# A six-layer windowed attention: query norms moved into the exponentials, masks in 64x32 tiles, x turned by one transpose, feed-forward weights loaded later, and a new order of stages

## The chip, the cores and the metric

One core of one Trainium2 chip runs the whole program. The metric is the device time of one execution in microseconds, as the median of a few runs. TensorE (PE), VectorE (DVE), ScalarE (ACT), GpSimd (POOL) and the DMA queue that SyncE (SP) feeds work side by side. They wait for each other by semaphores only.

## The reference

`x` has 16 batches of 128 rows of 128 numbers. A cross attention, a mixture of experts and a second cross attention come first. Most of the work is in what follows, six layers of local attention and a gated feed-forward part:

```python
def attn_layer(x, Wqkv, qs, ksc, Wo):
    q, k, v = jnp.split(x @ Wqkv, 3, -1)          # 16 heads of 64
    q = l2norm(q) * qs
    k = l2norm(k) * ksc
    q = q * cos * scale + rotate_half(q) * sin * scale
    k = k * cos * inv + rotate_half(k) * sin * inv
    return local_attention(q, k, v) @ Wo           # windows of 32 rows, each sees itself and the one before
for i in range(DEPTH):                             # 6
    x = attn_layer(shift_tokens(x), Wqkv[i], ...) + x
    x = ffn_layer(shift_tokens(x), ln_g[i], ...) + x
```

`shift_tokens` moves columns 64 to 127 down by one row. `l2norm` divides each head's row by its norm.

## The kernel before

**Units and slots.** A layer's attention is 64 units: 16 batches times 4 groups of four heads. Each engine has a list of stages, `(skew, function)`, and in slot c it runs each stage for unit c - skew, in the order of the list. Slots 0 to 7 of a layer are written out (`start`, mixed into the feed-forward part of the layer before), slots 8 to 63 are a loop of seven iterations with eight slots each (`steady`), and the last seven slots are written out again (`finish`), mixed into the layer's own feed-forward part. So there are 42 iterations of that loop in all. An engine runs its slot strictly in order; `wait_ge` makes it wait.

**One unit.** PE turns x once per batch (`l_turn_x`, every fourth slot, L802 and L803: two products, one with the identity and one with a shifted identity, which also does `shift_tokens`), ACT copies it out of PSUM and DVE takes the rest (`xs_part`, a high and a low part). PE projects queries and keys into bank 0 (`l_project_qk`, L814) and values into bank 1 (`l_project_v`, L823), with three products each. ACT squares bank 0 (L1186), DVE sums the squares (L1594) and multiplies bank 0 with the rotary tables (L1580, L1584). POOL adds the two halves (`l_add`, L530), finds the inverse norms in four small steps (`l_norm`, from a guess that ACT makes with Ln and Exp, L1192 and L1197) and multiplies queries and keys by them (`l_scale`, L551). PE turns the result in bank 2 (`l_turn_qk`, L831), ACT copies it out (L1202), and PE makes the scores in banks 3 and 4 (`l_scores`): first two products of the identity with the mask, in bf16 over the whole array (L850), then 16 products in tiles of 64 rows by 32 columns (L858). DVE takes the negated maxima (L1602), ACT makes four exponentials with them as bias (L1166), PE turns these (`l_turn`, L841), ACT copies them (L1174), PE multiplies them with the values in 64x32 tiles (`l_pv`, L878), DVE divides (L1617, L1619), PE turns the result (`l_turn_o`, L888), ACT copies it (L1208), and PE multiplies it with Wo (`l_output`, L898). Matrix products in fp32 stand in the trace as two records each.

**Values moved by DMA.** A product in a 64x32 tile reads its weights and data from the same half of the partitions. So for each pair of units SP waits for `v_done` and copies parts of `l_v` to other partitions (`move_values`, four DMAs, L360), and `l_pv` waits for them (`moved`).

**SP's order.** In each layer SP serves the moves, the next x (`take_x`, one DMA) and, at the start of a layer, the next projection weights. At a layer's end it loads Wo and the first two x of the next layer, waits until all four groups of the feed-forward part are done (`y_done`), and loads the next layer's feed-forward weights (`load_feed_forward`, 12 DMAs, L336 to L347) before it comes to the first moves.

Of the kernel before, what the change touches and what calls it, by code (L numbers as in the profile page):

```python
# [90 lines left out]
def build(nc, t, out):  # L91
    with ExitStack() as ctx:
# [31 lines left out]

        l_mask = sb("l_mask", [128, 2 * BAND], BF16)
# [88 lines left out]
        l_rn = sb("l_rn", [128, 2, 8])  # L214
# [52 lines left out]
        l = stage_sems("l_", core.replace("sub_done ", "") + "w_high_done w_split "  # L267
# [18 lines left out]
        def _(sp):  # L286
# [21 lines left out]
            for w in range(WINDOWS):  # L308
                first = max(w - 1, 0) * WINDOW
                rows = slice(w * WINDOW, (w + 1) * WINDOW)  # L310
                for p in range(2):
                    sp.dma_start(l_mask[rows, p * BAND:(p + 1) * BAND],
                                 t["const_bf"][rows, 128 + first:128 + first + BAND]).then_inc(ld_c, 16)
# [49 lines left out]
            def take_x(ly, b, k):  # L363

                sp.dma_start(xin[:, k], one(Y, b)).then_inc(ld_xin[k], 16)
# [6 lines left out]
            def serve_layer(ly, last):  # L372

                for b in range(4):
                    for q in range(2):
# [16 lines left out]
                if not last:  # L392
# [13 lines left out]
            load_feed_forward(0)  # L406
# [16 lines left out]
        def _(pool):  # L423
# [5 lines left out]
            pool.memset(l_ss[:, :, :, 1:], 1e-24).then_inc(preset, 1)  # L429
# [93 lines left out]
            def attention(ly):  # L523
# [8 lines left out]
                def l_norm(u, b, j):  # L532
# [11 lines left out]
                    pool.tensor_tensor(l_rn[:, k], t, y, ALU.mult).then_inc(l["rn_done"], 1)  # L544

                def l_scale(u, b, j):
# [3 lines left out]
                    v = l_qk[:, k].rearrange("p (h n) -> p h n", n=L_DIM)  # L550
                    pool.tensor_tensor(v, v, l_rn[:, k, :, None].broadcast_to([128, 8, L_DIM]),  # L551
                                       ALU.mult).then_inc(l["qk_done"], 1)

                return Pipeline(pool, [(4, l_norm), (3, l_add), (4, l_scale)], UNITS, UNROLL, 4)
# [36 lines left out]
        def _(pe):  # L591
# [180 lines left out]
            def attention(ly):  # L772
# [11 lines left out]
                def values_read(mine, b, r):  # L784

                    v, x = (issued(mine, fn, r) for fn in (l_project_v, l_turn_x))
                    pe.wait_ge(l["v_done"], upto(ub, no_more(4 * b + v, UNITS)))
                    pe.wait_ge(l["x_split"], upto(bb, no_more(b + (x + 3) // 4, B)))

# [5 lines left out]

                def l_turn_x(u, b, j):

                    if j % 4 == 0:
                        x = xin[:, j // 4]
                        pe.wait_ge(ld_xin[j // 4], (ly * B + b - j // 4) * 8 + 16)  # L800
                        values_read(l_turn_x, b, 0)
# [16 lines left out]
                def l_project_v(u, b, j):  # L818
                    g = j % 4
                    pe.wait_ge(l["x_split"], upto(bb, b + 1))  # L820
                    values_read(l_project_v, b, j % 4)
# [5 lines left out]
                def l_turn_qk(u, b, j):  # L827
                    pe.wait_ge(l["qk_done"], upto(ub, u + 1))
                    pe.wait_ge(l["qkT_done"], upto(ub, u))
# [15 lines left out]
                def l_scores(u, b, j):  # L845
# [963 lines left out]
```

## Time and profile before

| what | value |
|---|---|
| median of three runs | 2391.66 us (2388.51 to 2394.93) |
| the profiled execution | 2385.23 us, span of the core 2383.4 us |
| mean granted clock of TensorE | 0.968 of full speed |
| busy share PE, DVE, ACT, POOL | 93%, 72%, 66%, 59% |

The span runs from the first to the last instruction on the core. A busy share is an average over parts with different limits, so it doesn't name the bound of a part. The layers begin at about 570 us and take some 307 us each.

### The profile page before, as it was taken

How to read it: one execution, taken by the hardware profiler on the slowest of the kernel's cores; microseconds unless marked ns; L12 is line 12 of the kernel's file. 1: busy time of each engine (PE TensorE's matmuls, PEld its weight loads, DVE VectorE, ACT ScalarE, POOL GpSimd, SP SyncE). 2: the span in 40 equal slices, each digit the busy share in tenths (PEclk: the TensorE clock that was granted, in tenths of full speed). 3: DMA queues.
4: the chain of work that ended last, by engine and by line, in shares of the span. 5: the costliest groups of instructions: out<-in, count | busy, mean ns of one | idle time of the engine just before them, and what ended most of it. 6: DMA issues, size and time to landing. Idle time of an engine off the chain costs nothing.

```text
span 2383.4 us, 105405 instructions
## 1 busy us (share of the span) xinstructions
PE 2211.0 (93%) x36645; PEld 1694.9 (71%) x36645; DVE 1725.2 (72%) x4617; ACT 1563.0 (66%) x5192; POOL 1412.3 (59%) x2638
## 2 busy tenths in 40 slices
PE   6998699998999979999799998999988999889998
PEld 4775277776888658886578875788756888578885
DVE  4777788886777657786577865677756788568884
ACT  3554455565888548886478873788746888468883
POOL 3443611115888538885378863688726888278882
PEclk9998899998999989999999999999998999999999
DMA  3000000011111112111111111211102111021110
GB/s 98 0 0 1 0 1 0 0 48 43 49 39 40 31 42 54 40 40 33 43 50 40 40 29 34 63 40 39 34 21 71 40 39 38 14 50 40 40 38 22
DMA packets 107749, 82.51 MB, mean 35 GB/s; under 512 B 26422, under 2 KB 100292, under 8 KB 107588
## 3 DMA queue, kind: packets, MB, share of 16 engines
q1 hardware_dynamic: 107588, 80.46, 12.9%
q8 instruction: 89, 1.46, 0.3%
q14 instruction: 72, 0.59, 0.1%
HBM read 21.94 MB, written 1.05 MB: 10 GB/s over the span
## 4 chain that ended last, share of the span: by engine, by line
PE 74%; DVE 4%; issue 4%; SPq 2%; ACT 1%; POOL 1%; DMA 0%; DVEq 0%; ACTq 0%; POOLq 0%
PE bank L814 14%; PE bank L831 9%; PE bank L898 7%; PE bank L878 6%; PE bank L858 6%; PE bank L823 6%; PE bank L888 4%; PE bank L841 3%; PE bank L850 2%; PE bank L749 2%; PE bank L955 2%; PE bank L944 2%; PE bank L945 2%; PE bank L738 2%; PE bank L597 1%
## 5 line engine op out<-in xcount | busy, mean ns | idle before, releaser
L530 POOL TENSOR_TENSOR l_qk<-l_rot 128x512 f32<-128x512 f32 x384 | 494.4, 1287 | 134.0 <-PE bank L831 60.6
L1202 ACT ACTIVATE l_qkT<-bank 128x512 f32<-128x512 f32 x384 | 229.8, 599 | 278.2 <-PE bank L831 278.2
L1580 DVE TENSOR_TENSOR l_rot<-bank,l_tab 128x512 f32<-128x512 f32 x384 | 265.0, 690 | 197.8 <-ACT l_sq L1186 197.8
L551 POOL TENSOR_TENSOR l_qk<-l_qk,l_rn 128x512 f32<-128x512 f32 x384 | 400.9, 1044 | 0.9
L1166 ACT ACTIVATE prob<-bank,peak 128x64 f32<-128x64 f32 x1536 | 355.0, 322 | 1.3 <-DVE peak L1602 1.3
L814 PE MATMUL bank<-w_high,xs_part 128*128 128x512 f32 x768 | 351.8, 458 | 3.2 <-DVE xs_part L1571 2.8
L1186 ACT ACTIVATE l_sq<-bank 128x512 f32<-128x512 f32 x384 | 237.1, 617 | 55.9 <-PE bank L814 44.8
L1584 DVE TENSOR_TENSOR l_rot<-bank,l_tab 128x512 f32<-128x512 f32 x384 | 261.5, 681 | 0.0
L831 PE MATMUL bank<-const,l_qk 128*128 128x128 f32 x1536 | 255.2, 289 | 5.3 <-POOL l_qk L551 5.2
L1594 DVE TENSOR_REDUCE l_ss<-l_sq 128x8 f32<-128x512 f32 x384 | 259.8, 677 | 0.2
L898 PE MATMUL bank<-l_wo,l_oT 128*128 128x128 f32 x1536 | 239.0, 279 | 0.0
L823 PE MATMUL bank<-w_high,xs_part 128*128 128x256 f32 x768 | 202.9, 286 | 11.6 <-issue 11.6
L878 PE MATMUL bank<-l_v,probT 64*32 64x65 f32 x4608 | 179.5, 225 | 35.2 <-DMA stash<-l_v 22.8
L898 PEld LDWEIGHTS bank<-l_wo,l_oT 128*128 128x128 f32 x1536 | 206.3, 193 | 3.3 <-issue 0.3
L1602 DVE TENSOR_REDUCE peak<-bank 128x4 f32<-128x256 f32 x384 | 160.8, 419 | 50.7 <-PE bank L858 43.4
L831 PEld LDWEIGHTS bank<-const,l_qk 128*128 128x128 f32 x1536 | 163.5, 142 | 41.4 <-POOL l_qk L551 6.8
L878 PEld LDWEIGHTS bank<-l_v,probT 64*32 64x32 f32 x4608 | 117.2, 108 | 105.3 <-issue 105.3
L814 PEld LDWEIGHTS bank<-w_high,xs_part 128*128 128x128 f32 x768 | 146.8, 191 | 62.2 <-issue 5.8
L435 POOL TENSOR_SCALAR ln_rs<-ln_mv 128x1 f32<-128x1 f32 (+1 forms) x64 | 14.5, 227 | 273.5 <-DVE ln_mv L1548 128.3
L858 PE MATMUL bank<-l_qkT 64*32 64x64 f32 x12288 | 175.8, 223 | 0.0
L878 PE MATMUL bank<-stash,probT 64*32 64x65 f32 x7680 | 174.5, 226 | 0.0
L1619 DVE TENSOR_TENSOR o<-bank,rsum 128x256 f32<-128x256 f32 x384 | 163.1, 425 | 13.3
(202 smaller groups left out, 5374.8 us busy)
## 6 DMA issues: line engine op xcount, KB each, us to landing
stash<-l_v SPq DMA_DIRECT2D x768, 65.0 KB, 2.0
early<-in_L_ffn_Wqkv_dram SPq DMA_DIRECT2D x36, 256.0 KB, 3.2
xin<-Y SPq DMA_DIRECT2D x96, 64.0 KB, 1.8
l_wo<-in_L_ffn_Wo_dram SPq DMA_DIRECT2D x6, 512.0 KB, 3.8
f_w<-in_L_ffn_W_dram SPq DMA_DIRECT2D x6, 341.0 KB
out_dram<-X SPq DMA_DIRECT2D x4, 256.0 KB, 2.3
f_w<-in_L_ffn_W_dram SPq DMA_DIRECT2D x6, 128.0 KB
l_oT<-in_L_xattn_Wkv_dram SPq DMA_DIRECT2D x1, 512.0 KB, 6.1
```

The source lines that it names most:

```text
L530: pool.tensor_tensor(l_qk[:, k], l_rot[:, k, 0], l_rot[:, k, 1], ALU.add).then_inc(l["add_done"], 1)
L551: pool.tensor_tensor(v, v, l_rn[:, k, :, None].broadcast_to([128, 8, L_DIM]), ALU.mult).then_inc(l["qk_done"], 1)
L814: ins = pe.matmul(bank[:, 0, :].rearrange("p (q n) -> p q n", q=2), xs_part[:, part, j // 4], w[:, 0:2, 256 * g:256 * g + 256], start=n == ...
L823: ins = pe.matmul(bank[:, 1, 0:256], xs_part[:, part, j // 4], w[:, 2, 256 * g:256 * g + 256], start=n == 0, stop=n == 2)
L831: ins = pe.transpose(bank[:, 2, n * 128:(n + 1) * 128], l_qk[:, j % 2, n * 128:(n + 1) * 128], ident)
L858: ins = pe.matmul(bank[w * WINDOW:(w + 1) * WINDOW, 3 + r, BAND * p:BAND * (p + 1)], l_qkT[rows, j % 2, queries:queries + WINDOW], l_qkT[r ...
L878: ins = pe.matmul(bank[w * WINDOW:(w + 1) * WINDOW, 6 - p, at:at + L_DIM + 1], probT[rows, j % 2, 128 * r + w * WINDOW:128 * r + (w + 1) * ...
L898: ins = pe.matmul(bank[:, 7, 256:384], l_oT[:, j // 4, p], l_wo[:, p], start=p == 0, stop=p == 7, skip_group_check=True)
L1166: ins = act.activation(prob[:, k, n * BAND:(n + 1) * BAND], bank[:, 3 + r, p * BAND:(p + 1) * BAND], ACT.Exp, bias=peak[:, k, n:n + 1])
L1580: dve.tensor_tensor(l_rot[:, k, 0].rearrange("p (q h n) -> p q h n", q=2, h=4), bank[:, 0, :].rearrange("p (q h n) -> p q h n", q=2, h=4), ...
L1584: dve.tensor_tensor(l_rot[:, k, 1].rearrange("p (q h s n) -> p q h s n", q=2, h=4, s=2), bank[:, 0, :].rearrange("p (q h s n) -> p q h s n ...
L1594: dve.tensor_reduce(l_ss[:, k, :, 0], l_sq[:].rearrange("p (h n) -> p h n", n=L_DIM), AX.X, ALU.add)\
```

## The change

1. **Query norms.** POOL's `l_scale` multiplies the keys alone, 128x256 in place of 128x512. The queries' inverse norms go into the exponentials: ACT's four `ACTIVATE`s get a `[128, 1]` scale operand beside the bias. DVE writes the negated maxima into spare columns of bank 3 and multiplies them by the inverse norms in a new small instruction (`l_shifts`). `l_rn` has four buffers instead of two, and the last step of `l_norm` waits for `exp_done` of four units before.
2. **Mask in tiles.** The two whole-array mask products become eight products in the same 64x32 tiles as the scores, each with 64 rows of the identity and 128 columns of the mask.
3. **x.** The DMA of x does the shift: two DMAs per batch. PE turns x with one transpose into bank 2, columns 384 to 511, where `l_turn_qk` also writes; each of the two waits until the other's result is read.
4. **Feed-forward weights** of a layer are loaded inside that layer, after the moves of batch 3.
5. **Order.** New stage lists on PE, ACT, DVE and POOL. Scores move from skew 5 to 4, values, squares and rotation from 1 to 2, POOL's add from 3 to 4.

```diff
             def take_x(ly, b, k):
-                sp.dma_start(xin[:, k], one(Y, b)).then_inc(ld_xin[k], 16)
+                x = one(Y, b)
+                sp.dma_start(xin[:, k, 0:HALF], x[:, 0:HALF]).then_inc(ld_xin[k], 16)
+                sp.dma_start(xin[1:, k, HALF:], x[0:S - 1, HALF:]).then_inc(ld_xin[k], 16)
...
                             load_projections(ly + 1, 2 * b + q)
+                load_feed_forward(ly)
                 with sp.Fori(2, B // 2 - 1) as i:
...
                         take_x(ly + 1, b, b)
-                    sp.wait_ge(f["y_done"], upto(0, (ly + 1) * 4))
-                    apart(sp)
-                    load_feed_forward(ly + 1)
...
-                return Pipeline(pool, [(4, l_norm), (3, l_add), (4, l_scale)], UNITS, UNROLL, 4)
+                return Pipeline(pool, [(4, l_add), (4, l_norm), (4, l_scale)], UNITS, UNROLL, 4)
...
-                        pe.matmul(bank[0:HALF, 1, 256:384], x[:, 0:HALF], ident, start=True, stop=True)
-                        pe.matmul(bank[HALF:, 1, 256:384], x[:, HALF:], shift_t, start=True, stop=True)\
-                          .then_inc(l["x_turned"], 1)
+                        pe.wait_ge(ld_xin[j // 4], (ly * B + b - j // 4) * 16 + 32)
+                        turns_read(l_turn_x, b, 0)
+                        pe.transpose(bank[:, 2, 384:512], xin[:, j // 4], ident).then_inc(l["x_turned"], 1)
...
-                    for r in range(2):
-                        pe.matmul(bank[:, 3 + r, 0:2 * BAND], ident_bf, l_mask[:], start=True, stop=False,
-                                  skip_group_check=True)
+                    apart(pe)
+                    for w in range(WINDOWS):
+                        for r in range(2):
+                            rows = slice(64 * r, 64 * r + 64)
+                            at = 64 * r + min(w, 1) * WINDOW
+                            pe.matmul(bank[w * WINDOW:(w + 1) * WINDOW, 3 + r, 0:2 * BAND],
+                                      ident_bf[rows, at:at + WINDOW], l_mask[rows], start=True, stop=False,
+                                      skip_group_check=True)
...
-                stages = [(5, l_scores), (4, l_turn_qk), (6, l_pv), (1, l_project_qk), (1, l_project_v), (7, l_output), (6, l_turn_o), (5, l_turn), (0, l_turn_x)]
+                stages = [(4, l_turn_qk), (2, l_project_v), (6, l_pv), (7, l_output), (0, l_turn_x),
+                          (1, l_project_qk), (4, l_scores), (5, l_turn), (6, l_turn_o)]
...
                                                  bank[:, 3 + r, p * BAND:(p + 1) * BAND], ACT.Exp,
-                                                 bias=peak[:, k, n:n + 1])
+                                                 bias=peak[:, k, n:n + 1],
+                                                 scale=l_rn[:, j % 4, 2 * p + r:2 * p + r + 1])
...
+                return Pipeline(act, [(1, l_copy_x), (2, l_square), (3, l_log), (6, l_copy_prob), (7, l_copy_o),
+                                      (3, l_guess), (4, l_copy_qk), (5, l_exp), (2, l_copy_v)], UNITS, UNROLL, 4)
...
+                    dve.tensor_reduce(peaks, scores, AX.X, ALU.max, negate=True).then_inc(l["peaked"], 1)
+
+                def l_shifts(u, b, j):
+                    dve.wait_ge(l["peaked"], upto(ub, u + 1))
+                    dve.wait_ge(l["rn_done"], upto(ub, u + 1))
                     dve.wait_ge(l["exp_done"], upto(ub, u - 1))
...
+                                      l_rn[:, j % 4, 0:4].rearrange("p (b a) -> p a b", a=2), ALU.mult)\
+                       .then_inc(l["shifts_done"], 1)
```

On PE, one slot of the loop without an x, before; the nine rows of `l_pv` (L878) are cut to the first two:

```order
L850 MATMUL bank<-l_mask,cbf 128x128 x2
L858 MATMUL bank<-l_qkT 32x64 x16
L831 MATMUL bank<-const,l_qk 128x128 x4
L878 MATMUL bank<-l_v,probT 32x65
L878 MATMUL bank<-stash,probT 32x65
...
L814 MATMUL bank<-w_high,xs_part 128x512
...
L823 MATMUL bank<-w_high,xs_part 128x256
...
L898 MATMUL bank<-l_wo,l_oT 128x128 x2
L888 MATMUL bank<-const,o 128x128 x2
L841 MATMUL bank<-const,prob 128x128 x2
```

The same slot of the change (its line numbers: L834 is `l_turn_qk`, L826 `l_project_v`, L886 `l_pv`, L906 `l_output`, L817 `l_project_qk`, L857 and L866 `l_scores`, L844 `l_turn`, L896 `l_turn_o`):

```order
L834 MATMUL bank<-const,l_qk 128x128 x4
L826 MATMUL bank<-w_high,xs_part 128x256
...
L886 MATMUL bank<-l_v,probT 32x65
L886 MATMUL bank<-stash,probT 32x65
...
L906 MATMUL bank<-l_wo,l_oT 128x128 x2
L815 REGISTER_ALU
L817 MATMUL bank<-w_high,xs_part 128x512
...
L857 MATMUL bank<-l_mask,cbf 32x128 x8
L866 MATMUL bank<-l_qkT 32x64 x16
L844 MATMUL bank<-const,prob 128x128 x2
L896 MATMUL bank<-const,o 128x128 x2
```

There are two tiled blocks in a slot in both. Behind them stood `l_turn_qk` and `l_project_qk`; now `l_output` and `l_turn` do, and the masks are inside the tiled block. The scores of a unit now come in the slot in which it is turned.

On SP, between the last layer's end and the first moves of the next, before (the DMAs of `f_w`, `f_g` and `f_b` in the middle are cut):

```order
L333 DMA l_wo<-in_L_ffn_Wo_dram 128x8x128
L396 ISA
L365 DMA xin<-Y 128x128 x2
L400 ISA
L336 ISA
L336 DMA f_w<-in_L_ffn_W_dram 128x682
...
L347 DMA f_b<-in_L_ffn_b_dram 128x128
L411 REGISTER_ALU
L411 COMPARE_AND_BRANCH
L360 DMA stash<-l_v 64x260 x4
```

In the change these DMAs stand behind the moves (L361) of batch 3, ahead of the loop over the later batches:

```order
L361 DMA stash<-l_v 64x260 x4
L372 REGISTER_ALU
L368 DMA xin<-Y 128x64
L369 DMA xin<-Y 127x64
L355 REGISTER_ALU
L361 DMA stash<-l_v 64x260 x4
L337 ISA
L337 DMA f_w<-in_L_ffn_W_dram 128x682
```

What moved is the whole group of 12 loads, from ahead of a layer's first moves to behind its eighth group of moves.

## Rows read from the trace of the kernel before

**Rows 1.** The page's first part: busy time, share of the span, instructions

```profile
PE 2211.0 (93%) x36645; PEld 1694.9 (71%) x36645; DVE 1725.2 (72%) x4617; ACT 1563.0 (66%) x5192; POOL 1412.3 (59%) x2638
```

**Rows 2.** Windows: stretch, us, busy (x) PE PEld DVE ACT POOL, PEclk, DMA share, GB/s

```profile
950.02:980.21 30.19, 30.02 (x681) 24.30 (x682) 24.12 (x61) 24.58 (x91) 24.73 (x49) 1.00 0.15 40
```

**Rows 3.** Timeline of PE, one slot without x: start us, us, instruction

```profile
999.56 0.50 PE L814 MATMUL bank<-w_high,xs_part 128*128 128x512 f32 x1
999.89 0.40 PE L814 MATMUL bank<-w_low,xs_part 128*128 128x512 f32 x1
...
1000.36 0.28 PE L823 MATMUL bank<-w_high,xs_part 128*128 128x256 f32 x1
...
1000.71 0.61 PE L898 MATMUL bank<-l_wo,l_oT 128*128 128x128 f32 x4
...
1001.37 0.38 PE L841 MATMUL bank<-const,prob 128*128 128x128 f32 x2
1001.59 0.28 PE L850 MATMUL bank<-l_mask,cbf 128*128 128x128 bf16 x2
1001.79 0.45 PE L858 MATMUL bank<-l_qkT 64*32 64x64 f32 x32
1002.18 0.66 PE L831 MATMUL bank<-const,l_qk 128*128 128x128 f32 x4
...
1002.77 0.24 PE L878 MATMUL bank<-l_v,probT 64*32 64x65 f32 x1
...
1003.16 0.50 PE L814 MATMUL bank<-w_high,xs_part 128*128 128x512 f32 x1
```

**Rows 4.** Timeline of PE around the turn of an x

```profile
997.30 0.38 PE L841 MATMUL bank<-const,prob 128*128 128x128 f32 x2
...
997.98 0.28 PE L850 MATMUL bank<-l_mask,cbf 128*128 128x128 bf16 x2
```

**Rows 5.** ACT and DVE in the same slot (timeline), and two ACT lines' durations

```profile
999.77 0.92 ACT L1166 ACTIVATE prob<-bank,peak 128x64 f32<-128x64 f32 x4
...
1001.41 0.24 ACT L1197 ACTIVATE l_y<-l_y 128x8 f32<-128x8 f32 x1
1001.57 0.38 ACT L1208 ACTIVATE l_oT<-bank 128x256 f32<-128x256 f32 x1
1001.85 0.38 ACT L1174 ACTIVATE probT<-bank 128x256 f32<-128x256 f32 x1
1002.87 0.60 ACT L1202 ACTIVATE l_qkT<-bank 128x512 f32<-128x512 f32 x1 [0.64 <-PE bank L831]
...
1003.42 0.18 DVE L1617 RECIPROCAL rsum<-bank 128x4 f32<-128x4 f32 x1
...
L1166 ACT ACTIVATE prob<-bank,peak 128x64 f32<-128x64 f32 x1536 | 355.0, 322 | 1.3 <-DVE peak L1602 1.3
...
L1227 ACT ACTIVATE f_ge<-bank,f_b x72: 682/687/689, 814.0 to 2374.8; 128x512 f32<-128x512 f32 x48, 85x512 f32<-85x512 f32 x24
...
L1219 ACT ACTIVATE f_nT<-bank,f_g x24: 771/777/778, 807.8 to 2365.3; 128x512 f32<-128x512 f32 x24
```

**Rows 6.** POOL's scaling, a group of the page (count | busy, mean ns)

```profile
L551 POOL TENSOR_TENSOR l_qk<-l_qk,l_rn 128x512 f32<-128x512 f32 x384 | 400.9, 1044 | 0.9
```

**Rows 7.** Waits over the span: waiting line and its releaser, total us, times, longest

```profile
PE bank L878 <- DMA stash<-l_v: 22.8, 5, 4.9
```

**Rows 8.** SP's timeline and the chain at the start of layer 1

```profile
862.77 0.35 SPq L336 DMA_DIRECT2D f_w<-in_L_ffn_W_dram  x1
...
870.28 2.43 SPq L360 DMA_DIRECT2D stash<-l_v  x4
...
872.12 2.07 DMA stash<-l_v
...
886.81 0.28 PE L850 MATMUL bank<-l_mask,cbf 128*128 128x128 bf16 x2 [4.10 <-issue]
```

**Rows 9.** Windows: PE between its two waits at the start of layer 1 (columns: rows 2)

```profile
874.30:882.70 8.40, 8.38 (x126) 6.64 (x126) 4.22 (x11) 3.87 (x12) 3.09 (x6) 0.63 0.49 138
```

More of the change, by code:

```diff
@@ L307, in _ @@
             sp.dma_start(c_wo, t["L1_xattn_Wo"].rearrange("(c p) n -> p c n", p=128)).then_inc(ld_c, 16)
[L308 to L313, printed above, removed]
+            for r in range(2):
+                for w in range(2):
+                    rows = slice(64 * r + w * WINDOW, 64 * r + (w + 1) * WINDOW)
+                    for p in range(2):
+                        sp.dma_start(l_mask[rows, p * BAND:(p + 1) * BAND],
+                                     t["const_bf"][w * WINDOW:(w + 1) * WINDOW, 128:128 + BAND]).then_inc(ld_c, 16)
             for k, n in enumerate(("gamma_x", "beta_x", "gamma_l", "beta_l")):
@@ L374, in serve_layer @@
                 for b in range(4):
+                    if b == 2:
+                        sp.wait_ge(f["y_done"], upto(0, ly * 4))
+                        apart(sp)
                     for q in range(2):
@@ L820, in l_project_v @@
                     pe.wait_ge(l["x_split"], upto(bb, b + 1))
-                    values_read(l_project_v, b, j % 4)
+                    pe.wait_ge(l["v_done"], upto(ub, u))
                     for n, (part, w) in enumerate(passes):
@@ L828, in l_turn_qk @@
                     pe.wait_ge(l["qk_done"], upto(ub, u + 1))
-                    pe.wait_ge(l["qkT_done"], upto(ub, u))
+                    turns_read(l_turn_qk, b, j % 4)
                     for n in range(4):
@@ L848, in l_scores @@
                     pe.wait_ge(l["exp_done"], upto(ub, u))
-                    for r in range(2):
-                        pe.matmul(bank[:, 3 + r, 0:2 * BAND], ident_bf, l_mask[:], start=True, stop=False,
-                                  skip_group_check=True)
+                    apart(pe)
+                    for w in range(WINDOWS):
+                        for r in range(2):
+                            rows = slice(64 * r, 64 * r + 64)
[3 more added lines that the diff above has]
+                                      skip_group_check=True)
                     for p in range(2):
@@ L1007, in _ @@
             pe.wait_ge(c["kvT_done"], upto(0, B))
-            pe.wait_ge(c["v_done"], upto(0, 2 * B))
             first.start(0)
@@ L1011, in _ @@
             pe.wait_ge(c["evac_done"], upto(0, UNITS))
+            pe.wait_ge(c["v_done"], upto(0, 2 * B))
             first.start(1)
@@ L1154, in l_copy_x @@
                         act.wait_ge(l["v_proj"], upto(ub, u - 4))
-                        act.activation(xs_part[:, 0, j // 4], bank[:, 1, 256:384], ACT.Copy)\
+                        act.activation(xs_part[:, 0, j // 4], bank[:, 2, 384:512], ACT.Copy)\
                            .then_inc(l["x_high_done"], 1)
@@ L1570, in l_split_x @@
                         dve.wait_ge(l["x_high_done"], upto(bb, b + 1))
-                        dve.tensor_tensor(xs_part[:, 1, k], bank[:, 1, 256:384], xs_part[:, 0, k].bitcast(F32), ALU.subtract)\
+                        dve.tensor_tensor(xs_part[:, 1, k], bank[:, 2, 384:512], xs_part[:, 0, k].bitcast(F32), ALU.subtract)\
                            .then_inc(l["x_split"], 1)
@@ L1627, in l_residual @@
                         dve.tensor_tensor(one(Y, b), one(Y, b), bank[:, 7, 256:384], ALU.add).then_inc(l["res_done"], 1)
-                return Pipeline(dve, [(1, l_split_x), (5, l_peaks), (2, l_sum_squares), (6, l_divide), (2, l_floor), (7, l_residual), (1, l_rotate)],
+                return Pipeline(dve, [(1, l_split_x), (5, l_peaks), (5, l_shifts), (2, l_rotate), (6, l_divide),
+                                      (2, l_sum_squares), (7, l_residual), (2, l_floor)],
                                 UNITS, UNROLL, 4)
```

35 lines of the change are left out of this document (17 added, 18 removed).

## The prediction, made before the changed kernel ran

> **What bounds the kernel now.** I read the page's first part first: PE is busy for 93% of the span and no other engine for more than 72% [rows 1]. That is an average, so next come the windows of one iteration of the loop, eight units long: 30.19 us, of which PE is busy for 30.02, with the clock at its upper level (granted 1.00, that is 2.4 GHz); DVE is busy for 24.12, ACT for 24.58, POOL for 24.73 [rows 2]. So in the loops, 42 x 30.19 = 1268 us of the span, PE is the bound and the others have some 5.5 us of 30 to spare. What counts there is how long PE's slot is, from start to start. PE's timeline gives it [rows 3]: from the first product of L814 at 999.56 to the next at 1003.16, 3.60 us: L814 0.80, L823 0.35, L898 and L888 together 0.66 (L888 is two transposes like L841, 0.22, so L898 0.44), L841 0.22, the masks L850 0.20, the scores L858 0.39, L831 0.59, L878 0.39. An x, every fourth slot, adds 0.46: from L841 to L850 it takes 0.68 instead of 0.22 [rows 4, 3]. Eight slots and two x make 29.72, the other 0.47 of an iteration lies at its branch and at small waits, and I leave it as it is.
>
> Outside the loops, the table of waits shows one wait that comes once at each of five layer starts: L878 for the moved values, 22.8 us in all [rows 7]. The timeline of SP tells why: from 862.77 on it issues the feed-forward weights, and the first moves come at 870.28; their landing, 872.12 and 2.07 us more, is what the chain goes through [rows 8]. Behind that wait PE works at a granted 0.63 for 8.40 us, so for a good part at the lower level, 1.2 GHz [rows 9]. Then it stands still again for 4.10 us at the entry of the loop, where it waits for nothing that the profile shows ("issue") [rows 8].
>
> **The change part by part.** The sum is made against the profiled execution, 2385.2 us with a span of 2383.4; the median of the runs shown is 6.4 us higher, 2391.7.
>
> *x by one transpose.* Two transposes of 128 columns take 0.22 us from start to start (L841 to L850) [rows 3], so one takes 0.11 where the x took 0.46 [rows 4]. Over four units that is 0.35 / 4 = 0.088 us less per unit. The second DMA per x goes on SP, which waits for `v_done` most of the time in the loop, and the new waits on bank 2 are met early: ACT copies bank 2 about 0.6 us after `l_turn_qk` ends, PE comes to the x 1.3 us after it (L823 0.35, L878 0.39, L898 0.44 and a switch). With that cover gone each would cost some tenths of a us per batch.
>
> *Masks in tiles.* The two masks take 0.20 to the scores [rows 3]. Of this I give 0.11 to the two products and 0.09 to the switch from whole array to tiles, since L831, four transposes that would take 0.44, needs 0.59 before the tiled L878: 0.06 for starting behind a tiled block and 0.09 for the switch. In the change the switch lies ahead of the masks and stays. Eight masks in eight different tiles should cost about a quarter of what the 32 records of L878 need without the tail, 0.39 - 0.15 = 0.24 [rows 3], so 0.06, and the gain is 0.05 per unit. From below they could be free (gain 0.11); from above each could take its 0.055 alone (0.44 in all, a loss of 0.33). I take 0.06, since the nearest rows are tiles of the same shape.
>
> The Trainium skill (TensorEngine Tiling, section Instruction Overhead) gives each matmul an overhead of about 60 cycles; by this the eight masks would cost 8 x 25 ns = 0.2 us as an estimate, and the change would gain 54 us less. The trace doesn't agree for tiles: 32 records of L878 start and drain within 0.39 us, 12 ns each [rows 3].
>
> *PE's order.* L814 takes 0.80 although its later products need 0.235 each (999.89 to 1000.36), so 0.10 goes to the start behind a tiled block [rows 3]. Now L814 follows an ordinary product and saves 0.10, L831 saves 0.06; L898 and L841 stand behind the tiled blocks and pay. L841 is like L831, 0.06; L898 lies between, 0.06 to 0.14, I take 0.10. Sum 0, bounds -0.04 and +0.04.
>
> So a unit takes 0.088 + 0.05 = 0.138 us less on PE, a slot without x 3.55. Over 384 units (336 in the loops, the rest at a layer's ends, where PE is nearly as full) this is 53 us.
>
> *ACT.* Four exponentials per unit get a second pointer operand. A 128x512 copy without any takes 0.60 (L1202), with one bias 0.687 (L1227), with bias and scale 0.777 (L1219) [rows 5]: 0.09 each, 0.36 per unit. ACT's busy time rises from 24.58 / 8 = 3.07 to 3.43, under PE's 3.55, and it has nothing else to gain. But its order matters, since there is a ring: `l_turn` (L841), copy of it, copy of o, guess, copy of bank 2, exponentials, scores of the next unit, `l_turn`. From starts in the timeline [rows 5]: copy_prob 0.28 (size of L1208, 1001.57 to 1001.85), copy_o 0.28, guess 0.16, L1202 0.50 (1002.87 to the exponentials 0.50 later), exponentials (0.92 - 0.32) / 3 = 0.20 apart now, 0.29 then, so 3 x 0.29 + 0.41 = 1.28; two hand-overs of 0.04. That makes 2.58. On PE masks 0.06, scores 0.39, L841 to its end 0.44: 0.89. The ring is 3.47 us long, 0.08 under PE's 3.55: hidden, but barely. Without that cover each 0.01 costs 0.01 x 384 = 4 us.
>
> The Trainium skill (ScalarE: Activation LUTs, What ACT_TABLE_LOAD costs) gives an ACTIVATE 186 ns plus 0.833 ns per element, 93 ns for each pointer operand, and an overlap of 93 ns. The 0.09 agrees with the rows, but by its formula 64 elements with two pointers start 0.33 us apart; the ring would be 0.13 longer, 3.60, and the time 19 us more than my sum, as an estimate.
>
> *DVE and POOL.* `l_shifts` is as small as the reciprocal L1617, 0.18 [rows 5], and waits for the maxima, so 0.2 to 0.3 more: DVE goes from 24.12 / 8 = 3.02 to at most 3.3. POOL's scaling goes from 1.04 [rows 6] to about half, the bounds being 0 and 1.04 saved; POOL is at 3.09 [rows 2] and falls to 2.6. Both stay behind PE. POOL's gain shows only in the last slots of a layer and the first of the next, where PE has less to do: 2 us in all, by judgement.
>
> *Feed-forward weights.* Without them SP reaches the first moves as soon as the values are there: the 22.8 us go. Behind them, of the 8.40 us at 0.63 the same rows at the upper level would take 5.6 (0.39 for L878, 1.15 for L814 and L823, 0.44 for L888 and L841, then one slot of 3.60), so 2.8 lost there; I take 2 for each of five, 10 us. Back go waits of the kind that slots 4 and 5 have, 0.8 per layer, 4 us. Net 29. The 4.10 at the loop's entry stays. In the new place the 12 loads (862.77 to 870.28, 7.5 us) delay a pair of moves: values of the pair come 7.1 us after those of the one before, whose moves take 2.4, so the next start 2.8 late and land about 7.3 us after `v_done`; PV needs them nearly 10 us after it. Hidden, with 2.5 us to spare.
>
> Sum: 53 + 2 + 29 = 84 us. 2385.2 - 84 = 2301 for a profiled execution, 2391.7 - 84 = 2308 for the median.
>
> **The rivals.**
> A. ACT's ring binds (chance 0.15). For it: 0.08 of slack is thin, and slots with an x add a 0.28 copy. Against: ACT's sum is only 3.43. If a unit takes 3.65 instead of 3.55, 38 us are lost: 2346.
> B. The stall at the layer start stays in another form, because values are now projected a slot later, or the loads at batch 4 make PV wait (0.12). For: the margin is 2 to 3 us. Against: SP's queue is empty there. Then 29 us turn into 5: 2332.
> C. The other side: the eight masks don't overlap (0.09). If each takes 0.055 alone, a unit is 0.33 - 0.088 = 0.24 longer, 93 us, less 31 for the rest: 2391.7 + 62 = 2454. It decides from about 0.28 us for the eight on. Against it speak the rows of L878.
> D. The change doesn't do what it says in the loops, since something not on PE, such as DVE's longer slot, sets the pace near 3.60 (0.05): only the 29 and some of x remain, 2355.
> The forecast, PE-bound loops and the stall gone: 0.59.
>
> **How the numbers follow.** The forecast's own range: masks 0.03 to 0.15, L898 0.04 either way, stall and clock 20 to 38, so 2285 to 2335. The whole one reaches to A and B and part of D: 2282 to 2352. A measurement here can tell about 0.3%, 7 us, from no change. A, B and the forecast are faster, D mostly so: faster 0.88, within 0.3% 0.02, slower 0.10 with C.
>
> **What the changed profile would show.** An iteration of the loop of about 29.1 us, with PE busy for nearly all of it; from the first mask to the first score about 0.06; one record of 0.27 for an x; no wait of `l_pv` for the moves at a layer's start; exponentials of about 0.41 us; ACT busy for 27.5 per iteration. I would be wrong if PE showed regular gaps ahead of the masks (ring A), of `l_turn_qk` (POOL) or of L817 (DVE), or if the eight masks took over 0.2.

## The result, and the profile of the changed kernel

The changed kernel takes **2411.6 us** (median of 5 runs, 2411.2 to 2420.3) beside 2388.5 us of the kernel before on the same chip. The ratio is 1.010, with an interval of 1.0078 to 1.0122, so it is slower by 1%; 2308 was forecast. The profiled execution has a span of 2414.1 us.

First the page's busy times of the changed kernel, which answer to [rows 1]. PE is still the busiest (93% before); DVE went from 72 to 76% and ACT from 66 to 71%.

```profile
PE 2220.0 (92%) x38661; PEld 1677.6 (69%) x38661; DVE 1839.7 (76%) x5001; ACT 1722.8 (71%) x5192; POOL 1246.7 (52%) x2639
```

The window of the same stretch as in [rows 2] (columns as there; its width is my choice, an iteration is not exactly as long) shows what each engine does in the loop: PE is busy for 29.81 of 30.20 us, while ACT went from 24.58 to 27.80 and POOL from 24.73 to 21.11, about as forecast.

```profile
950.00:980.20 30.20, 29.81 (x724) 23.53 (x723) 26.61 (x69) 27.80 (x91) 21.11 (x49) 1.00 0.16 41
```

Next PE's timeline over one slot without an x. It answers to [rows 3]: from L817 to L817 it is 3.71 us (999.34 to 1003.05), where 3.55 was forecast. One slot can mislead, so the forecast is set against the trace term by term further down, in medians over many slots.

```profile
999.34 0.47 PE L817 MATMUL bank<-w_high,xs_part 128*128 128x512 f32 x1
...
1000.20 0.25 PE L857 MATMUL bank<-l_mask,cbf 64*32 64x128 bf16 x8
1000.27 0.53 PE L866 MATMUL bank<-l_qkT 64*32 64x64 f32 x32
1000.73 0.44 PE L844 MATMUL bank<-const,prob 128*128 128x128 f32 x2
1001.01 0.38 PE L896 MATMUL bank<-const,o 128*128 128x128 f32 x2
1001.22 0.60 PE L834 MATMUL bank<-const,l_qk 128*128 128x128 f32 x4
1001.58 0.36 PE L826 MATMUL bank<-w_high,xs_part 128*128 128x256 f32 x1
...
1002.19 0.21 PE L886 MATMUL bank<-l_v,probT 64*32 64x65 f32 x1
...
1002.58 0.71 PE L906 MATMUL bank<-l_wo,l_oT 128*128 128x128 f32 x4
1003.05 0.48 PE L817 MATMUL bank<-w_high,xs_part 128*128 128x512 f32 x1
```

The wait of `l_pv` for the moved values [rows 7] is gone. The table of waits shows another, which before did not have: `l_project_qk` (L817) waits for the rotation to give bank 0 free.

```profile
PE bank L817 <- DVE l_rot L1596: 46.4, 29, 3.7
```

Of these 29 waits, 15 with 33.6 us lie between the last exponentials of a layer and the first of the next, and 12 with 7.8 us in the three units behind them. The timeline at the start of layer 1 shows the longest. A unit's square is now a slot later than its projection, so ACT comes to it (869.68) only behind feed-forward work, the rotation follows, and the next projection stands still for 3.66 us.

```profile
869.68 0.60 ACT L1197 ACTIVATE l_sq<-bank 128x512 f32<-128x512 f32 x1
...
870.92 0.68 DVE L1596 TENSOR_TENSOR l_rot<-bank,l_tab 128x512 f32<-128x512 f32 x1
...
871.66 0.79 PE L817 MATMUL bank<-w_high,xs_part 128*128 128x512 f32 x1 [3.66 <-DVE l_rot L1596]
```

I measure a layer by its exponentials, one group of four per unit. The first four lines are of the kernel before, the others of the changed one. In the changed kernel the last of layer 0 start at 818.13 and the first of layer 1 at 882.93: a **boundary** of 64.8 us, where before had 57.6 (809.01 to 866.63). The **pace** in the loop, from the fourth unit of layer 1 (898.64) to the 59th (1108.17), is 209.53 / 55 = 3.81 us a unit, where before had 3.79 (889.05 to 1097.46).

```profile
809.01 0.94 ACT L1166 ACTIVATE prob<-bank,peak 128x64 f32<-128x64 f32 x4
866.63 0.92 ACT L1166 ACTIVATE prob<-bank,peak 128x64 f32<-128x64 f32 x4
...
889.05 0.72 ACT L1166 ACTIVATE prob<-bank,peak 128x64 f32<-128x64 f32 x3
...
1097.46 0.72 ACT L1166 ACTIVATE prob<-bank,peak 128x64 f32<-128x64 f32 x3
...
818.13 1.30 ACT L1176 ACTIVATE prob<-bank,peak,l_rn 128x64 f32<-128x64 f32 x4
882.93 1.29 ACT L1176 ACTIVATE prob<-bank,peak,l_rn 128x64 f32<-128x64 f32 x4
...
898.64 0.69 ACT L1176 ACTIVATE prob<-bank,peak,l_rn 128x64 f32<-128x64 f32 x2
...
1108.17 1.00 ACT L1176 ACTIVATE prob<-bank,peak,l_rn 128x64 f32<-128x64 f32 x3
```

PE also stands still at the end of a layer, where before had no such wait. There the masks (L857) stand still 17 times, 17.6 us in all, and the profile names no releaser. But each of these starts comes 0.10 us behind the end of the exponentials of the unit before, for which `l_scores` waits. In the loops the distance is never under 0.19. The longest waits have exponentials that are late themselves, since they wait for DVE (L1621), which comes to the maxima behind feed-forward work, 6 times and 6.7 us in all:

```profile
1121.29 1.29 ACT L1176 ACTIVATE prob<-bank,peak,l_rn 128x64 f32<-128x64 f32 x4 [1.11 <-DVE peak L1621]
...
1122.68 0.25 PE L857 MATMUL bank<-l_mask,cbf 64*32 64x128 bf16 x8 [2.10 <-issue]
```

### The profile page after: what moved, and what is told of

Same layout as the page of the kernel before. It is cut to its first block, busy times and chain, and to the rows that moved or that the text cites. A ratio compares the mean times of both kernels' runs of the same rounds, so it can differ in the third digit from the quotient of the medians.

```text
span 2414.1 us, 110102 instructions
## 1 busy us (share of the span) xinstructions
PE 2220.0 (92%) x38661; PEld 1677.6 (69%) x38661; DVE 1839.7 (76%) x5001; ACT 1722.8 (71%) x5192; POOL 1246.7 (52%) x2639
## 4 chain that ended last, share of the span: by engine, by line
PE 76%; issue 5%; DVE 4%; ACT 1%; POOL 1%; DVEq 0%; ACTq 0%; POOLq 0%
PE bank L817 12%; PE bank L906 10%; PE bank L834 7%; PE bank L886 7%; PE bank L844 6%; PE bank L866 6%; PE bank L826 5%; PE bank L896 4%; PE bank L857 3%; PE bank L756 2%; PE bank L964 2%; PE bank L953 2%; PE bank L954 2%; PE bank L745 2%; PE bank L604 1%
## 5 line engine op out<-in xcount | busy, mean ns | idle before, releaser
L1176 ACT ACTIVATE prob<-bank,peak,l_rn 128x64 f32<-128x64 f32 x1536 | 495.6, 412 | 6.7 <-DVE peak L1621 6.7
L817 PE MATMUL bank<-w_high,xs_part 128*128 128x512 f32 x768 | 343.8, 448 | 51.8 <-DVE l_rot L1596 46.4
L906 PE MATMUL bank<-l_wo,l_oT 128*128 128x128 f32 x1536 | 277.3, 304 | 0.0
L558 POOL TENSOR_TENSOR l_qk<-l_qk,l_rn 128x256 f32<-128x256 f32 x384 | 235.5, 613 | 55.1 <-POOL l_rn L550 0.2
L834 PE MATMUL bank<-const,l_qk 128*128 128x128 f32 x1536 | 237.4, 278 | 25.4 <-issue 25.1
L1213 ACT ACTIVATE l_qkT<-bank 128x512 f32<-128x512 f32 x384 | 228.9, 596 | 42.5 <-PE bank L834 41.8
L1615 DVE TENSOR_REDUCE bank<-bank 128x4 f32<-128x256 f32 x384 | 165.9, 432 | 118.2 <-PE bank L866 101.7
L826 PE MATMUL bank<-w_high,xs_part 128*128 128x256 f32 x768 | 237.5, 330 | 0.4 <-issue 0.4
L906 PEld LDWEIGHTS bank<-l_wo,l_oT 128*128 128x128 f32 x1536 | 204.3, 193 | 36.7 <-issue 1.9
L542 POOL TENSOR_TENSOR l_t<-l_s,l_y 128x8 f32<-128x8 f32 x384 | 77.3, 201 | 277.4 <-ACT l_y L1208 277.4
L866 PE MATMUL bank<-l_qkT 64*32 64x64 f32 x12288 | 205.7, 219 | 0.3 <-issue 0.2
L834 PEld LDWEIGHTS bank<-const,l_qk 128*128 128x128 f32 x1536 | 177.8, 142 | 39.0 <-issue 35.7
L817 PEld LDWEIGHTS bank<-w_high,xs_part 128*128 128x128 f32 x768 | 149.2, 194 | 79.4 <-DVE l_rot L1596 45.4
L886 PE MATMUL bank<-l_v,probT 64*32 64x65 f32 x4608 | 181.8, 224 | 14.3 <-ACT probT L1185 8.3
L1185 ACT ACTIVATE probT<-bank 128x256 f32<-128x256 f32 x384 | 147.8, 385 | 51.6 <-PE bank L844 33.2
L886 PEld LDWEIGHTS bank<-l_v,probT 64*32 64x32 f32 x4608 | 122.9, 107 | 79.5 <-issue 51.9
L886 PE MATMUL bank<-stash,probT 64*32 64x65 f32 x7680 | 176.5, 225 | 0.2
```

What stands on the lines that cost most here:

```text
L558: pool.tensor_tensor(v, v, l_rn[:, j % 4, 4:, None].broadcast_to([128, 4, L_DIM]), ALU.mult).then_inc(l["qk_done"], 1)
L817: ins = pe.matmul(bank[:, 0, :].rearrange("p (q n) -> p q n", q=2), xs_part[:, part, j // 4], w[:, 0:2, 256 * g:256 * g + 256], start=n == ...
L826: ins = pe.matmul(bank[:, 1, 0:256], xs_part[:, part, j // 4], w[:, 2, 256 * g:256 * g + 256], start=n == 0, stop=n == 2)
L834: ins = pe.transpose(bank[:, 2, n * 128:(n + 1) * 128], l_qk[:, j % 2, n * 128:(n + 1) * 128], ident)
L866: ins = pe.matmul(bank[w * WINDOW:(w + 1) * WINDOW, 3 + r, BAND * p:BAND * (p + 1)], l_qkT[rows, j % 2, queries:queries + WINDOW], l_qkT[r ...
L886: ins = pe.matmul(bank[w * WINDOW:(w + 1) * WINDOW, 6 - p, at:at + L_DIM + 1], probT[rows, j % 2, 128 * r + w * WINDOW:128 * r + (w + 1) * ...
```

## The experiments

Fourteen kernels, in four sets. Each ratio is to runs of the kernel before in the same set (medians 2388.6, 2390.8, 2388.5 and 2389.0 us).

**First set: which part costs the time.**

*Three parts without the others.* The kernel before with x by its DMA and one transpose (into bank 1), tiled masks and later feed-forward weights; its own orders, all norms on POOL.

> The kernel before, with its own stage order and its own norms, and three parts of the change: x shifted by its DMA and turned by one transpose (into bank 1, where it was), masks in 64x32 tiles, feed-forward weights loaded behind the moves of batch 3. Theory 1 (what made the change slow is in its order and its exponentials, a ring through ACT, while TensorE's own sum was right): PE stays the bound of the loops, a unit is 0.14 us shorter (0.088 for x, 0.05 for the masks), the 22.8 us of waits for the moved values go: 2388 - 53 - 25 = about 2310 us, 3.64 us per unit in the loops. Theory 2 (TensorE issues more instructions than it can dispatch, because of the eight masks): no gain in the loops or a loss, 3.78 us or more per unit, only the start of the layers is shorter: 2360 us or more.

2331.8 us, ratio 0.976 (0.974 to 0.978). So these parts gain 57 us, and what is left of the change, the query norms, the new orders and the move of x to bank 2, costs 80. Pace 3.76 (877.28 to 1084.18), boundary 56.4:

```profile
806.26 0.94 ACT L1171 ACTIVATE prob<-bank,peak 128x64 f32<-128x64 f32 x4
862.67 0.92 ACT L1171 ACTIVATE prob<-bank,peak 128x64 f32<-128x64 f32 x4
...
877.28 0.93 ACT L1171 ACTIVATE prob<-bank,peak 128x64 f32<-128x64 f32 x4
...
1084.18 0.92 ACT L1171 ACTIVATE prob<-bank,peak 128x64 f32<-128x64 f32 x4
```

*The change without the second pointer operand.* Queries are not normalised in this run.

```
-   bias=peak[:, k, n:n + 1], scale=l_rn[:, j % 4, 2 * p + r:2 * p + r + 1])
+   bias=peak[:, k, n:n + 1])
    # DVE's product in l_shifts: times l_v[:, 0, 0, 0:2, :, L_DIM] (ones) for l_rn[:, j % 4, 0:4]
```

> The changed kernel, but the exponentials take no scale operand, and the small product of DVE multiplies the maxima by ones, so that queries are not normalised; all waits stay. Theory 1 (ring through ACT and the scores): each exponential is 0.09 us shorter, the ring falls from 3.72 to 3.36 us, and the next bound takes over, PE's slot at about 3.6: loops near 3.65 us per unit instead of 3.81, 50 us less in all, about 2360 us. Theory 2 (TensorE's dispatch is the bound): nothing changes, 2411 us and 3.81 us per unit.

2411.0, ratio 1.009 (1.007 to 1.011): no change. Rival A, the ring through ACT, isn't what binds the changed kernel's loops. In the trace the masks start 0.3 us (median) behind the last exponential in the change, and 0.67 behind it here, at nearly the same pace (3.80).

*The change with whole-array masks.*

```
+   for r in range(2):
+       pe.matmul(bank[:, 3 + r, 0:2 * BAND], ident_bf, l_mask[:], start=True, stop=False, ...)
```

> The changed kernel with the two whole-array masks of before. Theory 1 (ring through ACT and the scores): the masks lie in the ring; from the first mask to the first score it takes 0.20 us with the switch instead of 0.067, so a unit is up to 0.13 us longer and the whole up to 50 us: 2430 to 2460 us. Theory 2 (TensorE's dispatch): 96 instructions fewer per iteration make it faster, by up to 30 us.

2414.1, ratio 1.0106 (1.0084 to 1.0127): not to be told from the change. Rival C falls, and so does a gain by the tiles. A slot of this run also shows that L817 takes 0.81 from its start to the masks (0.79 in the median), though no tiled block stands ahead of it:

```profile
1001.86 0.48 PE L817 MATMUL bank<-w_high,xs_part 128*128 128x512 f32 x1
...
1002.67 0.27 PE L853 MATMUL bank<-l_mask,cbf 128*128 128x128 bf16 x2
```

*The change with the feed-forward weights loaded at their old place.*

> The changed kernel with the feed-forward weights loaded where they were, ahead of a layer's first moves. Theory 3 (at a layer's start the wait for the moves was replaced by waits of the query and key projection for the rotation, which now comes a slot later): the moves are nearly hidden behind those waits, and the time rises by 0 to 10 us. Rival (the later loading is worth what I forecast, and the loss at the layer starts has another cause that adds to it): it rises by about 25 us.

2442.5, ratio 1.022 (1.020 to 1.0245). The later loads are worth 31 us inside the change, so the forecast's 29 stood and the theory that little of it was left fell.

**Second set: norms or orders.**

*The first set's best without the tiled masks.*

> The kernel before with x shifted by its DMA and the feed-forward weights loaded later; masks as two whole-array products. Theory 5 (masks in tiles gain nothing): in the trace of the run with all three parts the first mask comes 0.312 us after L841 instead of 0.218 and the scores take 0.461 instead of 0.385, which together cost 0.17 against the 0.14 that the masks themselves save, so 0.03 per unit too much; without the tiles the time is 10 us under 2332, about 2321. Rival (the prediction's term for the masks, a gain of 0.05 per unit): 2332 + 19 = 2351.

2332.5, ratio 0.9757 (0.974 to 0.977): the same as with tiles. Over all layers its loops are 8 us shorter (3.73 a unit in layer 1, 878.96 to 1084.33), and its boundaries 6 us longer, which the total evens out. Why the boundaries differ stays open. My theory of a loss of 10 us came true in the loops alone, and the forecast's gain of 19 missed. Why the tiles gain nothing on PE is in this slot of the run with tiles: from L841 to the first mask 0.32 instead of 0.22 [rows 3], masks 0.06 instead of 0.20, but the scores 0.46 instead of 0.39, in sum 0.84 for 0.81.

```profile
1004.25 0.38 PE L841 MATMUL bank<-const,prob 128*128 128x128 f32 x2
1004.57 0.25 PE L854 MATMUL bank<-l_mask,cbf 64*32 64x128 bf16 x8
1004.63 0.53 PE L863 MATMUL bank<-l_qkT 64*32 64x64 f32 x32
1005.09 0.65 PE L831 MATMUL bank<-const,l_qk 128*128 128x128 f32 x4
```

*The three parts and the query norms, orders of before.* `l_shifts` stands behind `l_peaks`; everything else of the norms is as in the diff.

> The kernel before with x by its DMA, tiled masks, later feed-forward weights and the query norms in the exponentials, all in the stage orders of before (plus the small product on DVE behind the maxima). Theory 4 (the new stage orders cost the time, the norms nothing): as the run without the norms, 2332, within 8 us. Rival (the norms cost it, through the exponentials or the longer way from maxima to exponentials): toward 2412.

2406.4, ratio 1.007 (1.006 to 1.0085). Against my theory: the norms alone cost 74.6 us. Pace 3.92 (894.31 to 1109.89). The table of waits and the timeline show where most of it lies in the loops. PE may turn an x (L805) into bank 1 only when ACT has copied the values (L1187) out of it. ACT copies them behind four exponentials, now longer, and a square:

```profile
PE bank L805 <- ACT l_v L1187: 18.5, 51, 1.0
...
1004.96 1.29 ACT L1173 ACTIVATE prob<-bank,peak,l_rn 128x64 f32<-128x64 f32 x4
1006.13 0.61 ACT L1194 ACTIVATE l_sq<-bank 128x512 f32<-128x512 f32 x1
1006.48 0.38 PE L842 MATMUL bank<-const,prob 128*128 128x128 f32 x2
1006.70 0.40 ACT L1187 ACTIVATE l_v<-bank 128x256 f32<-128x256 f32 x1
1007.16 0.33 PE L805 MATMUL bank<-const,xin 128*128 128x128 f32 x1 [0.30 <-ACT l_v L1187]
```

From L842 to the x it takes 0.68 here. The mean over the loops is 0.55, where the run without the norms has 0.23: 0.08 a unit, or 26 us in all, about half of what the loops lost. The turn of o behind L904 is late too in some slots (0.62 for 0.44), where DVE's division is late, but its mean rose by 0.02 only.

*The change without the query norms, new orders.*

> The change with its new stage orders, but all eight norms multiplied by POOL, no scale operand and no second step on DVE. Theory 4 (orders cost it): as the change, 2412, or more, since POOL's product is 0.4 us longer on the way to the turn of queries and keys. Rival (the norms cost it): toward 2332.

2407.6, ratio 1.008 (1.0065 to 1.009). The orders alone cost 76 us, and the norms in them 4 more. This run differs from the one with three parts also in that x is turned into bank 2, so the 76 us are those of orders and bank together. So both of my theories were half right, and the costs don't add: with the new orders the norms cost next to nothing, but the orders cost as much as the norms do in the old ones. Pace 3.81 (893.19 to 1102.79), boundary 62.9.

*Squares and rotations back in the slot of their projection, the rest of the change kept.*

```
-   DVE: [(1, l_split_x), (5, l_peaks), (5, l_shifts), (2, l_rotate), (6, l_divide), (2, l_sum_squares), ...]
+   DVE: [(1, l_split_x), (5, l_peaks), (5, l_shifts), (2, l_sum_squares), (6, l_divide), ..., (1, l_rotate)]
-   ACT: (2, l_square) second        + ACT: (1, l_square) last
-   POOL: (4, l_add), (4, l_norm)    + POOL: (4, l_norm), (3, l_add)
```

> The change with squares and rotations in the slot of their projection (skew 1, last on ACT and DVE, POOL adding at skew 3 ahead of the scaling), as before the change; PE's order and all the rest as in the change. Theory 6 (the boundary between layers is longer because the rotation and squares of a unit come a slot later and so behind feed-forward work; 7 us at each of five layers): from the last exponentials of a layer to the first of the next 57 us instead of 64, in all about 2412 - 35 = 2377, loops as in the change. Rival (PE's own new order makes the boundary): 2412.

2547.7, ratio 1.067. The boundary is 55.6 us, as the theory had it:

```profile
844.66 1.30 ACT L1176 ACTIVATE prob<-bank,peak,l_rn 128x64 f32<-128x64 f32 x4
900.30 1.29 ACT L1176 ACTIVATE prob<-bank,peak,l_rn 128x64 f32<-128x64 f32 x4
```

but the loops run at 4.3 a unit, which I hadn't foreseen. The table of waits names the cause: PE's turn of queries and keys (L834) waits for DVE to split x, 103.3 us in 90 waits, about one per x. Both use bank 2. The split stands behind DVE's rotation, which stands behind ACT's square, now last in its slot:

```profile
PE bank L834 <- DVE xs_part L1582: 103.3, 90, 1.7
...
1005.12 0.62 ACT L1197 ACTIVATE l_sq<-bank 128x512 f32<-128x512 f32 x1
...
1006.38 0.68 DVE L1595 TENSOR_TENSOR l_rot<-bank,l_tab 128x512 f32<-128x512 f32 x1
...
1006.97 0.28 DVE L1582 TENSOR_TENSOR xs_part<-bank,xs_part 128x128 fp32r<-128x128 f32 x1
...
1007.31 0.65 PE L834 MATMUL bank<-const,l_qk 128*128 128x128 f32 x4 [1.06 <-DVE xs_part L1582]
```

So the longer boundary goes with the later square and rotation. With x in bank 2 and PE's new order, taking them back costs more than it gives.

**Third set: single prices, and an order with one tiled block.**

*Later feed-forward weights alone.*

> The kernel before with the feed-forward weights loaded later and nothing else. The prediction's term: 29 us less, 2391 - 29 = 2362; what the run with x as well (2332) is below it is the one-transpose x, by the prediction 0.088 x 384 = 34 us, by the starts in the trace (0.482 for the slot's turn and x instead of 0.677, and 0.094 of the difference due to the tiled masks) 0.07 x 384 = 28 us. Rival (x is worth nothing, the loads all): 2332.

2354.2, ratio 0.986 (0.984 to 0.987): 34 us. The x is then 2354.2 - 2332.5 = 22, or 24 if each run is set against the kernel before of its own set.

*The change with `l_turn_qk` behind `l_project_v`, and ACT's exponentials ahead of its copy of bank 2.*

> The change with the turn of queries and keys between the projection of values and l_pv, and ACT's exponentials ahead of its copy of queries and keys. Theory 7 (the wait to enter a block of tiled products grows with the product before it: 0.22 us more behind the three 256-column products, 0.17 behind the 512-column ones, 0.15 behind four transposes): 0.07 per unit less, 27 us, about 2385. Rival (a slot is held by the chain through ACT, or entry costs the same behind anything): 2412 or more.

2464.1, ratio 1.031. It was to price the entry into the tiled block. The time goes to the turn of x, which waits for ACT's copy of queries and keys (L1213), now behind the exponentials: from L906 to L807 it takes 0.83 or 1.18 in most slots of the loops instead of 0.55. Slots without an x take 3.75 us in the mean, as in the change, so the gain that I expected of a cheaper entry isn't there: a rival's outcome.

*`l_pv` moved next to the scores, from the run with x and later weights.*

```
-   stages = [(5, l_scores), (4, l_turn_qk), (6, l_pv), (1, l_project_qk), ...
+   stages = [(5, l_scores), (6, l_pv), (4, l_turn_qk), (1, l_project_qk), ...
```

> The kernel before with x by its DMA and later feed-forward weights (2332), and l_pv moved right behind the scores, so that a slot has one block of tiled products instead of two. Theory 7: one entry (0.15) and one exit (about 0.1) less per unit, up to 0.25 x 384 = 96 us less, of which a wait for ACT's copies of the probabilities and of o may take 0.1 per unit: 2240 to 2290. Rival (entries and exits cost nothing of their own, or ACT's copies come too late by as much): 2332 or slower.

2542.4, ratio 1.064. The entry is cheaper, from L831 to the next 0.41 instead of 0.59, but `l_pv` now stands still for ACT's copy, which comes behind the copy of o. The timeline (ACT and PE) and the table of waits:

```profile
999.64 0.43 ACT L1208 ACTIVATE l_oT<-bank 128x256 f32<-128x256 f32 x1
...
999.91 0.44 ACT L1174 ACTIVATE probT<-bank 128x256 f32<-128x256 f32 x1
...
1000.49 0.21 PE L878 MATMUL bank<-l_v,probT 64*32 64x65 f32 x1 [0.66 <-ACT probT L1174]
...
PE bank L878 <- ACT probT L1174: 211.1, 280, 2.0
```

*The same with the turns ahead of the projection of values.*

> As the run before, and the turns of o and of the probabilities ahead of the projection of values, with ACT's exponentials ahead of its copy of queries and keys, so that the copies have more time before l_pv. Theory 7: 2235 to 2290. Rival (the turn now waits for the exponentials of its own slot): 2332 or slower.

2548.5, ratio 1.067. Now the turn of o waits for the division, and the exponentials wait for the maxima, as the table of waits shows. Both misses have one cause: I counted PE's slot and not the chain between two of its stages.

```profile
ACT prob L1166 <- DVE peak L1602: 295.5, 374, 2.8
...
PEld bank L888 <- DVE o L1619: 198.2, 290, 1.3
```

**Fourth set: what in the norms, what in the orders.**

*Norms in the orders of before, without the second pointer operand* (queries are not normalised).

> The run with the query norms in the orders of before (2406), with the exponentials' scale operand left out: DVE's small product multiplies the maxima by ones, so queries are not normalised, and every wait stays. Theory 8 (in the old orders the loop is a ring through ACT's exponentials, its square behind them and DVE's rotation, and the 0.36 us that four second operands add lie on it): back to about 3.75 us a unit, 2332 to 2345. Rival (the longer way from maxima over DVE's product to the exponentials does it): 2400.

2360.1, ratio 0.988 (0.986 to 0.9895); pace 3.81 (882.92 to 1092.47). Of the 74.6 us the operand makes 46, the rest of the norms (the longer way from the maxima over DVE to the exponentials among it) the other 28. The turn of x is back at 0.23 us behind L842 in the mean, so its wait for ACT's copy of the values, 26 us in the loops, came with the operand. The same operand costs nothing in the change, where x goes into bank 2.

*New orders without norms, PE's order as before.*

> The run with the new orders and all norms on POOL (2408), with the stage order of PE as before the change, those of ACT, DVE and POOL new. Theory 9 (what costs in the loops is PE's own new order, 0.05 a unit for entering tiled blocks; what costs at the boundaries is the squares' and rotation's later slot on ACT and DVE): loops 3.75 a unit instead of 3.81, from the last exponentials to the next first still 63 to 65 us, about 2385. Rival (PE's order makes the boundary): 57 us there. Rival (the old PE order doesn't fit the others, a wait in each slot): above 2408.

2698.1, ratio 1.129: the rival, a wait in each slot. PE's L816 stands still for the rotation, which the other engines' order puts a slot later. But the boundary is 64.4 us (65.8 in the mean of five), as long as with PE's new order, so PE's order isn't what lengthens it, and that half of my theory held. The table of waits, and the exponentials at the first boundary:

```profile
PE bank L816 <- DVE l_rot L1592: 246.4, 294, 5.1
...
864.97 0.94 ACT L1173 ACTIVATE prob<-bank,peak 128x64 f32<-128x64 f32 x4
...
929.40 0.92 ACT L1173 ACTIVATE prob<-bank,peak 128x64 f32<-128x64 f32 x4
```

So of the orders neither PE's nor that of squares and rotations could be taken back by itself without a loss. No run has the old boundary together with the loops' new pace.

## Why the prediction was wrong

The runs give this account, in medians: later weights -34, x -22, masks -1, new orders (with x in bank 2) +76, norms in these orders +4, together +23 us. Against the forecast of -84, the profiled execution is 115 us too long (107 by the medians). Of this some 49 lie in the loops, where 3.65 a unit was forecast and 3.80 came, and the other 66 at the layers' ends.

For the loops, here are the terms of a slot on PE without an x, from start to start, in medians over 306 slots of each trace. The masks' switch is in the row ahead of them.

| us | before | forecast | change | change, whole-array masks |
|---|---|---|---|---|
| L834 and L826, to `l_pv` | 0.94 | 0.88 | 0.89 | 0.89 |
| `l_pv` | 0.39 | 0.39 | 0.39 | 0.39 |
| L906 | 0.44 | 0.54 | 0.47 | 0.47 |
| L817 | 0.80 | 0.79 | 0.87 | 0.79 |
| masks | 0.20 | 0.06 | 0.07 | 0.21 |
| scores | 0.39 | 0.39 | 0.46 | 0.39 |
| L844 | 0.22 | 0.28 | 0.27 | 0.28 |
| L896 | 0.22 | 0.22 | 0.22 | 0.22 |
| sum | 3.60 | 3.55 | 3.65 | 3.64 |

- **Feed-forward weights: right.** 29 was forecast; alone they are worth 34, in the change 31.
- **x by one transpose: right in the change, less in the old orders.** An x adds 0.11 us to a slot of the change, as forecast, and added 0.47 before. In the old orders one transpose still adds 0.17 (0.39 from L841 to the masks for 0.22), and there 22 to 24 us came of the 34.
- **Masks in tiles: wrong in sign of the term, small.** The eight masks take 0.07 as forecast, the switch lies ahead of them as said (0.31 for 0.22 in the old order, 0.87 for 0.79 in the new), but the scores behind them went from 0.39 to 0.46, which the working held fixed. The gain of 19 us is nil. I haven't shown why the scores take longer.
- **"PE's order: sum 0": this step failed.** I read the 0.10 that L814 takes beyond its products as a start behind a tiled block, to be saved by moving it. It wasn't saved: with whole-array masks L817 follows an ordinary product and still takes 0.79, where 0.80 - 0.10 = 0.70 was to come. In return L906 behind the tiled block paid 0.03 and not 0.10. The switch itself is as large as I took it, 0.08 to 0.09, behind 512-column products as behind transposes. By the medians the order cost 0.04 a unit, at the upper bound that I gave, and the masks another 0.06 against their forecast. By the means a slot without an x went from 3.65 to 3.75: in half the slots `l_pv` comes some 0.08 to 0.12 later than in the others, as in the slot shown above. In about half of these ACT's copy of o, for which it waits, is later too. For the other half I have no cause.
- **"The rest at a layer's ends, where PE is nearly as full", and the orders of ACT, DVE and POOL costed at nothing: this step failed too.** Against the run with three parts, layer by layer from the starts of the exponentials over the whole trace: boundaries 33 us more, the last five units of the layers 18, the first three 6, the loops 20. The boundaries have the 33.6 us in which L817 waits for the rotation. The boundary is back at 55.6 us where squares and rotations are taken back, and stays at 64.4 where PE's order is. So rival B was near: a stall came at the layer's start in another form, but by the rotation, not by the values or the loads. The last units have the 17.6 us in which the masks wait for late exponentials.
- **DVE's slot (rival D): no.** Without the norms, and so without `l_shifts`, the loops keep their pace (3.81).
- **POOL's gain: nil.** POOL's scaling went from 1044 to 613 ns, its busy time by 3.6 us per window, but before the change PE didn't wait for POOL in the loops.
- **ACT's ring: right that it is hidden.** I worked out 0.08 of slack. In the change's loops the masks start 0.19 to 0.33 us behind the last exponential, and 0.10 where they do wait for it, so the slack is 0.1 to 0.2, and taking the operand away gained nothing. In the old orders the same operand costs 46 us, and 26 of them lie elsewhere: ACT comes later to its copy of the values, and the turn of x waits for that. I haven't followed the other 20. The cover that I called safe for x on bank 2 is real in the change, and goes in two of the runs with another order, at some 0.3 to 1.2 us per x.

The gains by weights and x were there, 56 us. The change spent them, and 23 us more, on new orders in which the norms cost little; but the norms only take work off POOL, an engine with time to spare. The version to keep is before with the three parts (2332), or without the tiled masks (2332.5); it beats both kernels by 2.4% and 3.3%.

## What to carry to other kernels

Before work is moved from one engine to another, ask whether the first is waited for; here it wasn't, and the orders in which the move fits cost 76 us. A table of stage skews is to be costed at the ends of its loop too, where a stage one slot later falls behind foreign work. A pipeline's slot on its busiest engine is a lower bound only: the three orders that I drew up by that sum alone ran into chains through other engines and came out 3 to 7% slower than before. Where two stages share a bank, such as x and the turn of queries and keys, a later reader on another engine holds up both.

## What the runs showed of the hardware

- A second pointer operand on a 128x64 exponential took the mean record from 322 to 412 ns and the group of four from 0.92 to 1.29 us, so 0.09 each, as forecast. The four start (1.29 - 0.41) / 3 = 0.29 us apart.
- Eight mask products in 64x32 tiles take 0.07 us to the first score, but the 32 score records behind them took 0.46 instead of 0.39 from start to start.
- Going from a product over the whole array to one in a 64x32 tile took 0.09 us more behind two 128-column transposes (0.31 for 0.22), and 0.08 behind products of 512 columns (0.87 for 0.79).
- PE started 0.10 us behind the end of the exponentials that it waited for (17 times the same).
- The same change costs much or nothing with what stands around it: the second operand 46 us or none, the query norms 74.6 or 4.
